# Moving GpSimd's logarithm corrections and the early router work of a fused decoder layer

## The reference

```python
x = layernorm(x + attn(x))                  # 16 heads of 16, causal, Wq Wk Wv Wo
x = layernorm(x + ssm(ctx, z=x))            # state space model over the context, gated by silu(x)
x = layernorm(x + moe(x))                   # 8 experts, the best 2 of a softmax, inner width 512
# ssm: u = silu(conv4(in_proj(ctx)));  dt, B, C = x_proj(u);  delta = softplus(dt_proj(dt) + b)
#   state[t] = state[t-1] * exp(delta[t] * A) + delta[t] * u[t] * B[t]       (256 channels x 16 states)
#   y[t] = sum over states of state[t] * C[t];  y = (y + D * u) * silu(z)
# moe: probs = softmax(x @ w_router);  top 2;  sum of prob * (silu(x @ w_gate[e] * 0.5) * (x @ w_up[e])) @ w_down[e] * 0.25
```

## Time and profile before

| | us |
|---|---|
| median of three runs | 419.07 (417.26 to 419.53) |
| the profiled execution | 420.82 |
| its span, first to last instruction | 419.1 |
| busy in the span: TensorE | 349.7 |
| VectorE | 251.7 |
| GpSimd | 236.4 |
| ScalarE | 209.1 |

### The profile page before, as it was taken

One profiled execution on the slowest core, in us unless ns is written; L12 is line 12 of the kernel. 1 busy time (PEld: TensorE's weight loads), 2 busy tenths in 40 slices (PEclk: granted clock), 3 DMA queues, 4 the chain that ended last, 5 costly groups with the idle time before them and its releaser, 6 DMA issues.

```text
span 419.1 us, 5802 instructions
## 1 busy us (share of the span) xinstructions
PE 349.7 (83%) x1846; PEld 207.2 (49%) x1846; DVE 251.7 (60%) x442; ACT 209.1 (50%) x488; POOL 236.4 (56%) x223
## 2 busy tenths in 40 slices
PE   8797768977787687877779586999999999999972
PEld 3453435634365344644436242566666666666551
DVE  3979998798978989797986664122222222222134
ACT  4577866858886787948870101222322222212103
POOL 3079999987798958977796204133332333322214
PEclk9999595998999989998996698999999999999988
DMA  7050021271127201251119911011111111111062
GB/s 216 7 104 3 25 52 40 49 238 33 45 69 200 79 32 37 81 199 38 52 31 366 369 38 29 23 50 50 40 48 41 50 50 41 47 41 38 27 214 100
DMA packets 29455, 34.47 MB, mean 82 GB/s; under 512 B 4074, under 2 KB 23826, under 8 KB 29426
## 3 DMA queue, kind: packets, MB, share of 16 engines
q1 hardware_dynamic: 24770, 26.36, 20.5%
q0 software_dynamic: 2208, 6.03, 4.8%
q10 hardware_dynamic: 2448, 1.71, 1.3%
HBM read 28.92 MB, written 5.18 MB: 81 GB/s over the span
## 4 chain that ended last, share of the span: by engine, by line
PE 37%; DVE 5%; ACT 3%; DMA 2%; POOL 2%; issue 2%; DVEq 0%; POOLq 0%; ACTq 0%
PE psS L1628 19%; PE psD L1647 5%; PE psO L1647 5%; PE psD L1638 2%; PE psS L1475 1%; PE psT L1623 1%; DMA c_rows<-z_out 1%; PE psS L1441 1%; POOL rstd L500 1%; ACT experts L686 1%; DVE u_sb L1144 1%; DMA delta<-x_rows,row_in 1%; PE psS L1685 1%; DMA z_out<-delta,row_out 1%; PE psT L1469 1%
## 5 line engine op out<-in xcount | busy, mean ns | idle before, releaser
L1628 PE MATMUL psS<-experts,delta 128*128 x184 | 86.5, 593 | 0.5 <-ACT delta L815 0.5
L511 POOL TENSOR_TENSOR experts<-experts,c_rows 128x1024 f32<-128x1024 f32 x31 | 73.3, 2364 | 19.2 <-DVE experts L981 18.7
L981 DVE TENSOR_TENSOR_SCAN experts<-experts,psD 128x512 f32<-128x512 f32 x64 | 74.3, 1202 | 0.1
L569 POOL DMA_INDIRECT z_out<-delta,row_out x23 | 22.7, 989 | 88.5 <-ACT delta L829 88.5
L1218 DVE COPY u_sb<-psD 128x512 f32<-128x512 f32 x23 | 15.9, 691 | 68.7 <-PE psD L1638 68.7
L686 ACT ACTIVATE experts<-delta,A_sb 128x255 f32<-128x255 f32 x128 | 54.7, 519 | 0.8 <-DVE du L926 0.8
L1392 PE MATMUL psT<-ident,probs_at 128*128 128x128 f32 x192 | 35.1, 312 | 22.8 <-ACT probT L724 22.8
L1628 PEld LDWEIGHTS psS<-experts,delta 128*128 128x128 f32 x184 | 33.1, 190 | 24.3 <-issue 23.3
L969 DVE TENSOR_TENSOR psD<-du,psD 128x512 f32<-128x512 f32 x64 | 41.1, 686 | 4.5 <-PE psD L1350 4.4
L1392 PEld LDWEIGHTS psT<-ident,probs_at 128*128 128x128 f32 x192 | 24.3, 157 | 32.8 <-ACT probT L724 31.8
L1226 DVE TENSOR_TENSOR du<-du,psS 128x512 f32<-128x512 f32 x23 | 15.8, 687 | 37.4 <-PE psS L1628 37.4
(11 more groups left out here) (243 smaller groups left out, 592.5 us busy)
## 6 DMA issues: line engine op xcount, KB each, us to landing
c_rows<-c_dram SPq DMA_DIRECT2D x32, 256.0 KB, 3.4
experts<-in_L_ffn_w_gate_dram SPq DMA_DIRECT2D x8, 512.0 KB, 6.0
experts<-in_L_ffn_w_up_dram SPq DMA_DIRECT2D x8, 512.0 KB, 7.0
experts<-in_L_ffn_w_down_dram SPq DMA_DIRECT2D x8, 512.0 KB, 8.1
x_in<-in_x_dram SPq DMA_DIRECT2D x4, 256.0 KB, 5.2
x_rows<-x_sb SPq DMA_DIRECT2D x4, 256.0 KB, 2.4
probs_at<-z_out SPq DMA_DIRECT2D x4, 256.0 KB, 4.9
c_rows<-z_out ACTq DMA_DIRECT2D x4, 256.0 KB, 5.9
```

The costliest lines, as they stand in the source:

```text
L511: pool.tensor_tensor(states[:, g % ST], states[:, g % ST], c_rows[:, g % CR].rearrange("p n (o s) -> p n o s", o=1).broadcast_to([P, 2, HA ...
L981: dve.tensor_tensor_scan(states[:, g % ST, n].rearrange("p h s -> p (h s)"), dA[:, g % DA, n].rearrange("p h s -> p (h s)"), psD[:, n, :], ...
L1628: ins = pe.matmul(psS[:, bank, :], xgT[:, s % 2, k, :], gate_up_of(bass.ds(e, 1), i)[:, k, :], start=(k == 0), stop=(k == FC - 1))
```

## The change

GpSimd does one split and two `fix_log` before its first product. `fix_log(2)` and `fix_log(3)` follow the products of steps 0 and 1 of batch 1, the second split those of step 2. VectorE does `finish_delta(2)` at step 4 and `finish_delta(3)` at step 6 of batch 1. SyncE loads expert 0 in batch 0, none in batch 1, 1 and 2 in batch 2 after waits for du and the split, 3 and 4 in batch 3.

In the tail VectorE's last product by C (`multiply_last`) goes ahead of the last residual; `add_last_state` keeps the two additions and waits for the deviation. The softmax of the known tiles goes before it, their indices beside the transposes of gated y, their ranks, tiles and places before the last logits. ScalarE's exponentials of the known tiles go ahead of its last norm. TensorE has 32, 10, 2 and 2 warm-ups instead of 16, 14 and 2, and ranks the known picks before it transposes x2 instead of after the logits.

```diff
 SyncE, in the loop over b and m
                     if m == 6:
-                        if b == 0:
+                        if b == 2:
                             sp.wait_ge(du_rdy, B)
-                        for e in range(EARLY * b // B, EARLY * (b + 1) // B):
+                            sp.wait_ge(bc_rdy, TH)
+                        for e in ((0,), (), (1, 2), (3, 4))[b]:
                             load_expert(e)
 GpSimd
-            for th in range(TH):
-                split_bc(th)
-            for b in range(B):
+            split_bc(0)
+            for b in range(BH):
                 fix_log(b)
...
                     if NP * b + m < STEPS - 1:
                         multiply_c(NP * b + m)
+                    if b == 1 and m <= 2:
+                        if m < B - BH:
+                            fix_log(BH + m)
+                        else:
+                            pool.wait_ge(y_sum, sums(NP * b + m + 1))
+                            split_bc(1)
 ScalarE, after the loop
-            normalise_rows(2 * (B - 1), x1_of(B - 1), 0, x1_rdy, 1)
-            half_tanh(B - 1)
             shifted_exponentials(0, 0, KNOWN)
+            normalise_rows(2 * (B - 1), x1_of(B - 1), 0, x1_rdy, 1)
+            half_tanh(B - 1)
 VectorE, in the loop
-                    if 0 < g < B:
-                        finish_delta(g)
+                    if g == 1:
+                        finish_delta(1)
+                    if b == 1 and m in (4, 6):
+                        finish_delta(m // 2)
...
                     elif m == 7:
+                        if b == B - 1:
+                            multiply_last()
                         residual(b)
 VectorE, after the loop
-            add_last_state()
             link(dve.memset(picks_b, 0.0))
             shift_logits(0, KNOWN)
+            largest(0, 0, KNOWN)
+            add_last_state()                # without the product; first waits for rstd_rdy, 2 * b + 1
             gating(B - 1)
             gate_output(B - 1)
+            find_picks(0, QC)
             add_gated(B - 1)
-            largest(0, 0, KNOWN)
+            find_picks(QC, KNOWN)
+            mark_picks(0, KNOWN)
             apply_last_norm()
-            pick_experts(0, KNOWN)
+            take_ranks(0, 0, KNOWN)
+            link(tiles_and_places(0, KNOWN))
+            mark_places(0, 0, KNOWN)
             take_logits(B - 1)
             shift_logits(KNOWN, NT)
-            take_ranks(0, 0, KNOWN)
             largest(1, KNOWN, NT)
-            pick_experts(KNOWN, NT)
-            link(tiles_and_places(0, KNOWN))
-            mark_places(0, 0, KNOWN)
+            find_picks(KNOWN, NT)
+            mark_picks(KNOWN, NT)
 TensorE, after the loop
-            keep_warm(16)
+            keep_warm(32)
             transpose_gated(B - 1)
-            keep_warm(14)
+            keep_warm(10)
+            rank_picks(0, 0, KNOWN)
+            keep_warm(2)
             transpose_x2(B - 1)
             keep_warm(2)
             route(B - 1)
-            rank_picks(0, 0, KNOWN)
             keep_warm(10)
             rank_picks(1, KNOWN, NT)
```

More of the change, by code:

```diff
@@ L110, in decoder_layer @@
     DA, ST, CR, PR = 3, 5, 4, 8
-    assert DM == P and DI == S == HID and QC == FC == HALVES == 2 and HD == 16 and BC == 32 and TH == 2
+    assert EARLY == 5 and DM == P and DI == S == HID and QC == FC == HALVES == 2 and HD == 16 and BC == 32 and TH == 2
     with ExitStack() as stack:
@@ L1052, in take_logits, with multiply_last @@
                                 psT[:, 0:QC * NE].rearrange("p (t e) -> p t e", t=QC)).then_inc(psT_taken, 1)
+            def multiply_last():
+                g = STEPS - 1
+                dve.wait_ge(scanned, 2 * STEPS)
+                dve.wait_ge(ld_c[g % CR], 16 * (g // CR + 1))
+                link(dve.tensor_tensor(states[:, g % ST], states[:, g % ST], c_rows[:, g % CR].rearrange(
+                    "p n (o s) -> p n o s", o=1).broadcast_to([P, 2, HALVES, S]), ALU.mult))
             for b in range(B):
@@ L1086, in add_last_state @@
                 g, b = STEPS - 1, B - 1
[L1087 to L1090, removed]
+                dve.wait_ge(rstd_rdy, 2 * b + 1)
                 link(dve.tensor_tensor(states[:, g % ST, 0], states[:, g % ST, 0], states[:, g % ST, 1], ALU.add))
@@ L1108, in largest, with find_picks, mark_picks @@
                 dve.drain()
-            def pick_experts(lo, hi):
-                n = hi - lo
+            def find_picks(lo, hi):
                 for t in range(lo, hi):
                     dve.max_index(top_idx[:, t], top_val[:, t], probs[:, t])
+            def mark_picks(lo, hi):
+                n = hi - lo
                 dve.drain()
@@ L1575, in _ @@
                         project_v(b + 1, 1, psS[:, 3, :])
-            keep_warm(16)
-            transpose_gated(B - 1)
-            keep_warm(14)
[L1579 to L1582, removed]
             def carry(out_ps, t):
@@ L1598, in rank_picks @@
                 ins.then_inc(rank_ps, 1)
+            keep_warm(32)
+            transpose_gated(B - 1)
+            keep_warm(10)
+            rank_picks(0, 0, KNOWN)
+            keep_warm(2)
+            transpose_x2(B - 1)
+            keep_warm(2)
+            pe.wait_ge(psT_taken, taken["x2T", B - 1])
+            route(B - 1)
             def invert_places():
```

## The result

The changed kernel takes 412.27 us (median of four runs, 411.86 to 415.32), the kernel before 418.16 (416.72 to 419.53): ratio 0.9855, 95% interval 0.9819 to 0.9890. In a second measurement the ratio was 0.9850 (0.9806 to 0.9894).

What follows compares the result with a forecast made beforehand. TensorE's untouched expert stage passes every earlier gain or loss on one for one; before it no engine is saturated. -2.5 + 4.1 - 4.4 = -2.8, with 0.4 taken back -2.4: off the median of 419.07, 416.7 us, range 412.8 to 420.6.

Steps and rivals of the forecast that it cites:

- +0.4 for the clock: Batch 1: TensorE idles about 3 us more and may fall to 1.2 GHz; 0.4 us of the gain taken back.
- step 2: Batch 0: VectorE loses finish_delta(2) and (3), 4.0 us; 1.6 counted as gain (0 to 3.0), not all being on the path.
- Step 1: Start: without the second split, VectorE's 0.98 us idle before finish_delta(0) nearly goes; gain 0.9.
- GpSimd's lateness in batch 0: Batch 0: GpSimd loses 11.4 us of work before its first product; counted as nothing, since scans look back five states.
- Step 3: Batch 1: the moved pairs cost 3.8 and 3.3 us, less slacks of 0.5 and 2.46; +4.1, between +1.0 and +5.5.
- just in time: End of batch 1: GpSimd's last products, though late, come when TensorE's closing sum wants them; GpSimd's lateness alone 0 to 1 us.
- The first rival: Batch 1: the moved operations fall into waits and cost only +1.0; 413.2 us in all; chance 0.20.
- The harshest reading: Batch 1: all four finish_delta operations blocked by a full GpSimd product, 4 x 2.73 = 10.9 us, batch +8; not adopted.
- Step 5: Tail: gain 2.9 up to the logits, 1.5 from ranking known tiles earlier; sum -4.4, between -2.5 and -5.0.
- the pile-up: Batch 1, steps 12 to 15: finish_delta meets full products, TensorE at half clock; batch +6.5, whole 421.1 us; chance 0.15.
- the too long warm-ups: Tail: 32 warm-ups at 1.2 GHz end 5 us after gated y; tail loses 0.7, whole 421.4 us; chance 0.10.

Runs made afterwards that it cites:

- e2: The kernel before with only the edits after the last scan (the new tail): ratio 0.9901 to the kernel before.
- e1: The kernel before with only the scan-stage edits (GpSimd's order, finish_delta(2) and (3) moved, SyncE's loads), old tail: ratio 0.9932 to the kernel before.
- e9: The changed kernel with three warm-up matmuls ahead of the first projection of u: ratio 0.9855 to the kernel before.
- e12: The changed kernel with finish_delta(1) ahead of scan(0) instead of at step 1: 411.87 us, ratio 0.9841 to the kernel before.
- e5: The changed kernel with a two-value copy in place of finish_delta(2) and (3), their logarithm left out: 412.47 us, ratio 0.9853.
- e11: The changed kernel with three warm-ups before the first projection of u and two-value copies in place of finish_delta(2) and (3): ratio 0.9808.
- e3: The kernel before with only VectorE's move of finish_delta(2) and (3) and SyncE's loads, GpSimd's order unchanged: ratio 0.9990 to the kernel before.
- e4: The changed kernel with GpSimd's old order (both splits and all four corrections ahead of the first product): 415.26 us, ratio 0.9916.
- e8: The kernel before, run again unchanged for a second profile: batch 0 took 48.14 us, batch 1 47.39.
- e7: The changed kernel, run again unchanged for a second profile: ratio 0.9850 to the kernel before.
- e6: The changed kernel with finish_delta(2) ahead of the maxima of step 2 of batch 1 instead of at step 4: 412.6 us.
- e10: The changed kernel with three warm-ups before the first projection of u and finish_delta(2) at step 2 of batch 1: 412.69 us.

## Why the prediction was wrong

The means of the profiles against my terms. Scan stage: before, the two and e2; changed, the two, e1 and e9. Tail and rest: before, the four with the old tail; changed, the ten with the new.

| | predicted | profiles |
|---|---|---|
| start | -0.9 | -1.1 (at equal clock: full -2.0, low -0.6 to -1.1) |
| batch 0 | -1.6 | -3.4 (48.15 to 44.72) |
| batches 1 and 2 | +4.1, +0.4 for the clock | +4.5 (95.90 to 100.42) |
| batch 3 | 0 | -0.1 |
| tail | -4.4 | -4.5 (34.24 to 29.74) |
| after the gather | 0 | -0.5 |
| sum | -2.4 | -5.1 (medians: -5.9) |

**The step that failed is step 2**, at the words "Of the 4.0 I let 1.6 through". 3.4 came through, above my upper bound of 3.0. I had reasoned that the maxima come from TensorE's scores, so that attention would hold back a part, and had set one share for both pairs. The reasoning holds at step 3, where `finish_delta(3)` indeed gave nothing: scan(3) to scan(4) is 6.98 before and 6.99 after. At step 2 it is false. There VectorE had a single wait of 0.55 us and 2.6 us of `finish_delta(2)`, and the whole pair was on the path, with that wait: scan(2) to scan(3) took 8.8 us in the three profiles without the move, 5.6 to 5.9 in all with it but e12's. With the 0.3 us that step 1 became longer, this is 2.9 of the 3.4. A part per step, not one share for both pairs, would have given it. The rest of batch 0 lies in steps 4 to 6, where TensorE's clock differs: the two executions of before are 1.1 us apart there.

Step 2 is 1.8 us of the miss. The profiles can't place all of the rest. By them start and batches together gain 0.1 us, by the median of e1 the scan stage gains 2.9 (1.6 to 4.1). The four changed profiles lay 0.8 us above their kernels' medians on average, those of before at theirs, which accounts for some of it; that batches 1 and 2 cost less in most executions than in these profiles would account for more, and the medians of e5 and e11 point that way, but it is not shown.

Step 1 was right in kind. The 0.98 us of idle time that I took as its bound came from an execution with TensorE's projection at 1.2 GHz: with it at full clock the same wait is 1.35 to 1.36 us (e3, e4, e8), and the first operation behind it also became shorter (1.09 to 0.74).

That GpSimd's lateness in batch 0 costs nothing was right for the kernel before, and stayed right only because GpSimd was moved too (e3, e4). I had not asked this of the edit.

Step 3 had the right size, and in the changed kernel and e7 the right path: 3.8 and 3.8 us for the pairs against 3.8 and 3.3, TensorE's 0.5 and VectorE's 2.46 of slack used up. In e1, e9 and e12 it came out near the same sum by luck: the first pair took 2.1, and the products that I had "just in time" for the closing sum of batch 1 were late, with the clock lost behind them. The first rival named the time (413.2), but the profiles do not show its way: batches 1 and 2 cost 3.8 us or more, not 1.0. The medians do not rule 1.0 out.

As the Trainium skill has it ("SBUF — State Buffer", "Who interferes with whom"), the blocked operation waits for GpSimd's to end. In the changed kernel all four end 0.55 us after one of GpSimd's. The harshest reading, four full waits of 2.73, was reached by one of four (2.74); the others met a shorter operation or the end of one (2.19, 1.65, 1.04).

Step 5 held within 0.5 us a term: deviation 1.6 us; the transposes of x2 begin 11.4 us after the residual instead of 14.8, the logits' copy 13.9 instead of 17.2; the last ranks follow the logits by 3.4 us instead of 4.6. From the residual to the first gather it is 25.3 to 25.6 us in all ten profiles with the new tail, 29.7 to 30.1 in the four without. A tail of 29.2 to 29.5 us goes with a last attention output of TensorE, ahead of the residual, of 2.8 to 3.5 us, one of 30.0 to 30.3 with 3.8. Neither the pile-up nor the too long warm-ups came: 32 took 7.07 us.

## What to carry to other kernels

Ask step by step, not batch by batch, which engine's queue is the path: look for the engine with almost no idle time in that step (VectorE had 0.55 us of 8.8 in step 2), and count an instruction that leaves it in full. Of an instruction that is added, count nothing until the wait there is used up (0.5 and 2.46 us in batch 1). When work is taken off one engine, ask again who was late behind it without being noticed: here moving VectorE's work was worth nothing until GpSimd's was moved too. A wait of TensorE can cost more than its length, if its clock is lost behind it: give it both prices. An instruction that may be blocked by another engine has no single price either: it costs what it meets, and that can differ between executions of the same program.

## What the runs showed of the hardware

The two operations of `finish_delta`, 128x512 with both inputs in SBUF, took 0.67 to 0.69 us alone and up to 2.82 beside GpSimd's, ending about 0.55 us after these ended; GpSimd's additions beside them took 1.6 instead of 1.27, its product 2.81 instead of 2.35. TensorE's clock took one of two courses at the same place of the same program: the second projection of u took 1.96 us in six profiles and 2.7 to 3.7 in the other eight. Where TensorE's closing sum had waited 1.73 to 1.80 us for GpSimd, it kept 2.4 GHz in three profiles (e4, e5, e11) and ran at 1.2 in one (e3); where it had waited 2.4 us, it lost the clock in all five (e1, e6, e9, e10, e12).
